# A four-layer modulated convolution: edge work of VectorE split in three, the scaled identity moved to ScalarE, the last weight set earlier

## What is computed

```python
def _layer(x, style, w, b, mw, mb, typ):
    s = style @ mw.T + mb
    weight = SCALE * w * s[:, None, :, None]
    demod = lax.rsqrt(jnp.sum(weight * weight, axis=(2, 3)) + EPS)
    weight = weight * demod[:, :, None, None]
    ...
out = x
for i, typ in enumerate(TYPES):   # ('same', 'upsample', 'same', 'downsample')
    out = _layer(out, style, weights[i], biases[i], mod_w[i], mod_b[i], typ)
x = x + out
```

## Time and profile before

| | before |
|---|---|
| median of 3 runs | 683.77 us (682.12 to 684.29) |
| the profiled execution | 683.69 us, span 681.9 us |
| TensorE matmul busy | 653.8 us (96%) |
| TensorE weight load busy | 622.7 us (91%) |
| VectorE busy | 558.8 us (82%) |
| GpSimd busy | 456.9 us (67%) |
| ScalarE busy | 354.6 us (52%) |
| chain that ended last | PE 57%, DVE 20%, issue 12%, ACT 6% |

### The profile page before, as it was taken

How to read it: one execution, slowest core, us unless ns; L and a number is a source line. 1 busy time by engine, 2 the same in 40 slices (tenths; PEclk the granted TensorE clock), 3 DMA queues, 4 the chain that set the end, 5 groups by cost and what they waited for, 6 DMA issues and landing times.

```text
span 681.9 us, 12957 instructions
## 1 busy us (share of the span) xinstructions
PE 653.8 (96%) x4771; PEld 622.7 (91%) x4771; DVE 558.8 (82%) x680; ACT 354.6 (52%) x610; POOL 456.9 (67%) x393
## 2 busy tenths in 40 slices
PE   8998999899999999998999999999989999999887
PEld 7798999899899999998989999999979899999886
DVE  6988788888898888798788888888889888888861
ACT  5354545654555655535655555566454565555441
POOL 3357677775778877657857777786577777777620
PEclk9998999999999999998999999999999999999999
DMA  7348877578778778886758888777787677988764
GB/s 251 63 102 209 209 168 198 146 196 193 173 197 193 193 192 207 197 192 171 175 165 206 213 185 201 185 187 192 175 223 172 153 196 195 216 194 205 184 170 126
DMA packets 146990, 125.63 MB, mean 184 GB/s; under 512 B 6064, under 2 KB 113648, under 8 KB 146928
## 3 DMA queue, kind: packets, MB, share of 16 engines
q1 hardware_dynamic: 146560, 124.56, 73.8%
q10 hardware_dynamic: 368, 0.25, 0.1%
HBM read 36.51 MB, written 33.75 MB: 103 GB/s over the span
## 4 chain that ended last, share of the span: by engine, by line
PE 57%; DVE 20%; issue 12%; ACT 6%; DMA 2%; SPq 1%; DVEq 0%; ACTq 0%; POOL 0%; POOLq 0%
PE po L200 9%; PE po L201 9%; PE po L202 9%; PE pg L202 4%; PE pg L200 4%; PE pg L201 4%; PE pm L200 4%; PE pm L202 4%; PE pm L201 4%; ACT xh L554 3%; DVE Wf L853 3%; DVE T L827 2%; PE pg L205 2%; PE pg L206 2%; DVE Wf L857 2%
## 5 line engine op out<-in xcount | busy, mean ns | idle before, releaser
L200 PE MATMUL po<-xh,W 128*128 128x256 f32 (+1 forms) x640 | 202.9, 317 | 7.6 <-issue 3.7
L201 PE MATMUL po<-xl,W 128*128 128x256 f32 (+1 forms) x640 | 201.7, 315 | 0.0
L202 PE MATMUL po<-xh,W 128*128 128x256 f32 (+1 forms) x640 | 200.9, 314 | 0.0
L818 DVE TENSOR_TENSOR xl<-X,xh 128x1290 fp32r<-128x1290 f32 x64 | 140.9, 2201 | 61.9 <-ACT xh L554 60.8
L200 PEld LDWEIGHTS po<-xh,W 128*128 128x128 f32 x640 | 126.9, 198 | 14.7 <-issue 9.3
L202 PEld LDWEIGHTS po<-xh,W 128*128 128x128 f32 x640 | 127.1, 199 | 6.2
L201 PEld LDWEIGHTS po<-xl,W 128*128 128x128 f32 x640 | 127.7, 200 | 5.3
L607 ACT CAST Gh<-Gf 128x512 fp32r<-128x512 f32 x64 | 39.6, 619 | 152.9 <-DVE Gf L849 152.9
L827 DVE SCALAR_TENSOR_TENSOR T<-po,DD,M 128x512 f32<-128x512 f32 x96 | 71.2, 742 | 32.2 <-ACT M L561 21.2
L750 POOL TENSOR_TENSOR Gl<-Gf,Gh 128x256 fp32r<-128x256 f32 x30 | 22.6, 754 | 103.1 <-ACT Gh L607 103.1
L554 ACT CAST xh<-X 128x1290 fp32r<-128x1290 f32 x64 | 87.8, 1372 | 7.4 <-POOL X L719 5.4
(11 more groups left out here) (175 smaller groups left out, 1786.2 us busy)
## 6 DMA issues: line engine op xcount, KB each, us to landing
X<-in_xin SPq DMA_DIRECT2D x64, 516.0 KB, 4.2
out<-T SPq DMA_DIRECT2D x64, 512.0 KB, 5.8
W<-W SPq DMA_DIRECT2D x93, 256.0 KB, 4.5
W<-W SPq DMA_DIRECT2D x31, 384.0 KB, 5.6
V<-V SPq DMA_DIRECT2D x32, 256.0 KB, 5.2
V<-W SPq DMA_DIRECT2D x32, 128.0 KB, 4.4
V<-Vx SPq DMA_DIRECT2D x32, 128.0 KB, 4.2
E<-in_ed SPq DMA_DIRECT2D x1, 768.0 KB, 7.3
```

Of the source, the lines that this page charges most:

```text
L200: eng.matmul(o, wh_, rh, start=first, stop=False)
L201: eng.matmul(o, wh_, rl, start=False, stop=False)
L202: return eng.matmul(o, wl_, rh, start=False, stop=last)
L818: tt(xl[:, n % XH, 0:w], X[:, n % XR, 0:w], r32(xh[:, n % XH, 0:w]), ALU.subtract).then_inc(s_xl, 1)
```

## The change

On VectorE, `edge` takes a third argument. Part 0 stands where all of it stood, at the end of sample 3's turn; part 1 at the end of the next group's sample 0, part 2 at the end of sample 0 another group later. On ScalarE a group's first turn begins with `x_high` of the odd tile and with the identity for the next group, then come the casts; `m_out` of sample 1 moves ahead of the cast of unit 6 (the last sum: three of W's five blocks). GpSimd loses the identity. In the table, group 29 does unit 3 of group 31 one sample earlier, and group 30 does units 4 to 6 of group 31 ahead of sample 0 instead of sample 1.

```diff
+         NGR - 3: [[(2, 0), (2, 1)], [(1, 4), (1, 5), (1, 6)], [(2, 2), (2, 3)], []],
+         NGR - 2: [[(1, 4), (1, 5), (1, 6)], [], [], []]}
...
+            def identity(g):
+                if g:
+                    act.wait_ge(s_ce, cnt(g - 1, 5))
+                for b in range(NG):
+                    m = act.activation(cols(ID[:])[:, b // 2, :, b % 2], EYE[:, 0:C], ACT.Copy,
+                                       scale=inv3[:, g * NG + b:g * NG + b + 1])
+                m.then_inc(s_id, 1)
...
             high(0, 3)
+            act.wait_ge(s_sc, SC_D)
+            identity(0)
             q3_high(1)
...
                 if i == 0:
-                    if b == 0:
-                        x_high(1)
-                    for x in units_of(b):
-                        high(*x)
-                    if b:
-                        x_high(2 * g + 1)
+                    x_high(2 * g + 1)
+                    if g + 1 < NGR:
+                        identity(g + 1)
+                    highs(b, (0, 1, 2, 3, 4, 6))
...
                     t_out(b - 1)
-                    for x in units_of(b):
-                        if x[1] != 5:
-                            high(*x)
+                    highs(b, (0, 1, 4))
                     m_out(b)
+                    highs(b, (6,))
+                    sums_behind(b)
...
-            def identity(g):
-                if g:
-                    pool.wait_ge(s_ce, cnt(g - 1, 5))
-                pool.tensor_tensor(cols(ID[:]), EYE[:, 0:C].unsqueeze(1).unsqueeze(3).to_broadcast([128, 2, C, 2]),
-                                   bc2(gs(inv3, g), 1), ALU.mult).then_inc(s_id, 1)
...
-                if divmod(b - 1, NG) in edge_at:
-                    c, k = edge_at[divmod(b - 1, NG)]
-                    edge(c, k)
-                    if k == 3 and c + 1 < len(CHUNKS):
-                        edge_in(c + 1)
+                for part, back in ((0, 1), (1, 2), (2, 6)):
+                    if divmod(b - back, NG) in edge_at:
+                        edge(*edge_at[divmod(b - back, NG)], part)
```

More of the change, by code:

```diff
@@ L41 @@
 FIRST = {0: [[(1, 2), (1, 3)], [(2, 0), (2, 1)], [(1, 4), (1, 5), (1, 6)], [(2, 2)]],
-         1: [[(1, 3), (2, 0), (2, 1)]] + SLOTS[1:]}
+         1: [[(1, 3), (2, 0), (2, 1)]] + SLOTS[1:],
+         NGR - 3: [[(2, 0), (2, 1)], [(1, 4), (1, 5), (1, 6)], [(2, 2), (2, 3)], []],
+         NGR - 2: [[(1, 4), (1, 5), (1, 6)], [], [], []]}
 def shared(b):
@@ L652, in _, with highs, sums_behind @@
             q3_high(2)
+            def highs(b, part):
+                for x in units_of(b):
+                    if x[1] in part:
+                        high(*x)
+            def sums_behind(b):
+                if weights_at(b - 1):
+                    sums_high(weights_at(b - 1))
             for b in range(B):
@@ L678, in _ @@
                 elif i == 2:
[L679 to L682, removed]
+                    highs(b, (4, 6))
                     m_out(b)
@@ L685, in _ @@
                         x_high(2)
[L686 to L690, removed]
-                else:
[L692 to L695, removed]
+                    sums_behind(b)
+                    highs(b, (2, 3))
+                else:
+                    sums_behind(b)
+                    highs(b, (2, 3))
                     m_out(b)
@@ L765, in _ @@
             pool.wait_ge(s_sc, SC_D)
-            pool.wait_ge(s_in["eye"], 16)
-            identity(0)
             q3_full(1)
@@ L778, in _ @@
                         for x in units_of(b):
-                            low(*x)
-                    if g + 1 < NGR:
-                        identity(g + 1)
+                            if x[1] < 4:
+                                low(*x)
                 elif i == 1:
@@ L897, in edge_in, with edge @@
                 tt(XS[:, 0:n], XE[:, cs, :], bc(S[:, 0, cs], 8), ALU.mult).then_inc(s_ed, 1)
-            def edge(c, k):
+            def edge(c, k, part):
                 a, n = CHUNKS[c]
@@ L903, in edge @@
                 y1, y2 = Y1[:, 0:n], Y2[:, 0:n]
[L904 to L908, removed]
-                elif k == 1:
[L910 to L914, removed]
+                if part == 0:
+                    dve.wait_ge(s_e, 4 * c + k + 1)
+                    if k == 0:
+                        v = y1[:, :, 0:6]
+                        link(tt(v, got(0, 6), bc(b0z[:, cs], 6), ALU.add))
+                        tt(ZE[:, 0:n, 1:7], v, bc(D10[:, cs], 6), ALU.mult).then_inc(s_ed, 1)
+                    elif k == 1:
+                        tt(y1[:, :, 0:11:2], got(0, 6), bc(S[:, 1, cs], 6), ALU.mult)
+                        link(tt(y1[:, :, 1:10:2], got(6, 5), bc(S[:, 1, cs], 5), ALU.mult))
+                        link(dve.tensor_scalar(Y[:, 0:n, 1:12], y1[:, :, 0:11], bias(1), None, ALU.add))
+                    elif k == 2:
+                        link(tt(y1[:, :, 0:8], got(0, 8), bc(DD[:, P2, cs], 8), ALU.mult))
+                        link(dve.tensor_scalar(HH[:, 0:n, 2:10], y1[:, :, 0:8], bias(2), None, ALU.add))
+                    else:
+                        v = y1[:, :, 0:3]
+                        link(tt(v, got(0, 3), bc(DD[:, P3, cs], 3), ALU.mult))
+                        dve.scalar_tensor_tensor(out=EP[:, cs], in0=v, scalar=bias(3), in1=XE[:, cs, 1:4],
+                                                 op0=ALU.add, op1=ALU.add).then_inc(s_ed, 1)
+                elif part == 1:
+                    if k == 1:
+                        link(tt(y1[:, :, 0:11], Y[:, 0:n, 1:12], Y[:, 0:n, 0:11], ALU.add))
+                        link(tt(y2[:, :, 0:10], y1[:, :, 1:11], y1[:, :, 0:10], ALU.add))
+                    elif k == 2:
+                        link(tt(y1[:, :, 0:9], HH[:, 0:n, 1:10], HH[:, 0:n, 0:9], ALU.add))
+                        link(tt(y2[:, :, 0:8], y1[:, :, 1:9], y1[:, :, 0:8], ALU.add))
+                    elif k == 3 and c + 1 < len(CHUNKS):
+                        edge_in(c + 1)
+                elif k == 1:
@@ L918, in edge @@
                 elif k == 2:
[L919 to L923, removed]
                     link(tt(y1[:, :, 0:7], y2[:, :, 1:8], y2[:, :, 0:7], ALU.add))
@@ L926, in edge @@
                                              op0=ALU.mult, op1=ALU.mult).then_inc(s_ed, 1)
[L927 to L931, removed]
             def final():
```

## The result

The changed kernel takes **656.56 us** (median of 4 runs, 656.35 to 656.76), the kernel before 683.42 us on the same chip. The ratio is 0.9608 with a 95% interval of 0.9592 to 0.9625. The forecast was 659.4 us and the range 654 to 671. The profiled execution took 656.46 us, 654.7 of it span.

The account below looks back on a forecast made before the run. A loop through ScalarE and VectorE, a little longer than TensorE's work, stalls TensorE. Span 681.9 less 26.3 (19.89 middle, 6.37 end) plus 2.0 staying is 657.6; 1.8 more gives 659.4 us, range 654 to 671.

Parts of the forecast that it names:

- The loop: Groups 2 to 28: M, Q2h, xh, xl and W's differences take a little longer than TensorE's work, 18.85 us.
- Its size: Groups 2 to 28: 544.48 us less 524.59 is 19.89 us of stalls; 2.0 us set against the gain.
- low end: 654 us: no residue (657.4), edge-matmul overlap (1 us) and the half-clock stretch at 59.09 gone (1.7 us).
- ScalarE's row of steps: Each group from T0 + 1.2: xh 1.39, identity 1.15, Q2h to T 3.45 us; M at T0 + 8.3.
- xl and W: VectorE in each group: xl starts at T0 + 2.9, takes 2.21 us; W's differences end at T0 + 10.1.
- Counts as nothing: GpSimd: losing 32 identity operations, median 2.02 us, gains no time, since it is on nobody's path.
- The edges: Edge groups and those behind: 4.30 us of VectorE work, split into 1.48, 1.74 and 1.08 us, fits.
- The end: After 625.31 us: stalls of 2.07, 1.76, 0.83 and 1.71 us for half clock go, 6.37 us in all.
- The loop stays, shorter: Rival, 0.13: identities cost 0.40 us each, the loop stays the bound, some 0.5 us lost a group; 671 us.
- The wait moves: Rival, 0.05: W's crossing grows by 1 us or more and the stall shows up behind it; 676 to 683 us.
- last sign of being wrong: The crossing from the end of W's differences to the next plain convolution takes 9 us.
- The slower rival: Rival, 0.04: four identities hold up ScalarE's queue; gain lost from 2.7 us for four, 697 us at 0.8 each.

Follow-up runs that it names:

- m_ahead_only: Kernel before with M ahead of the second W cast and nothing else: 683.27 us, ratio 0.9991.
- xh_behind: Changed kernel with xh again behind the casts to Q2h and the identity behind xh: 676.13 us, ratio 0.9893.
- m_behind: Changed kernel with M of the second sample again behind the cast of unit 6: 656.60 us, ratio 0.9605.
- gpsimd_identity: Changed kernel with the identity on GpSimd again: 657.32 us, ratio 0.9620.
- xh_first_only: Kernel before with ScalarE casting xh of the odd tile ahead of Q2h and the other casts, nothing else: 668.86 us, ratio 0.9787.

## Why the prediction was right, step by step

**The loop.** Right, and the main point. In the changed kernel every group from 2 to 28 takes 18.85 us plus its edge matmuls, to within 0.1 us; with xh behind Q2h, in the same kernel, 19.3 us come back in the middle (542.19 against 522.85). That the loop goes through xh, xl and W, and not through M, is shown by m_ahead_only and xh_behind together; "M" here is that of the second sample. The M of the last sample, with which the prediction's loop starts, hangs on VectorE too, through Gf and the cast to Gh; the prediction took its time as fixed.

**Its size.** The step forecast 19.89 less a residue of 2.0. Measured: 21.63. Two terms were mis-sized. The residue was 0.13 us (groups 17 and 18), as W ended earlier than I thought. And the edge matmuls cost 13.9 us (522.85 less 508.95), not 15.64: their rows sum to 15.64 us in the changed kernel too, so 1.7 us of them lie beside their neighbours. The prediction had named 1 us of this overlap for its low end. It also named one half-clock stretch among the stalls' consequences where there were two; the sum is not touched, since it took the stretch as a whole.

**ScalarE's row of steps.** Identity 1.15 forecast, 1.07 measured for four (336 to 354 ns each, overlapping). M at T0 + 8.3 forecast, 7.98 measured, and not from ScalarE's work: it waits 1.30 us for TensorE. M's term in the argument was empty, since M behind the cast costs nothing either (m_behind).

**xl and W.** W's second difference was forecast at T0 + 10.1 and ended at 9.78. Three terms were off and nearly cancel. The start was kept at T0 + 1.2, the end of the last sample's M; in group 27 that M ends at T0 + 0.27, and xl starts at T0 + 1.90 instead of 2.9. xl, kept at 2.21, takes 1.76, because it starts ahead of GpSimd's differences now, and not behind them. And the 0.6 us allowed for TensorE's sums became waits of 1.09 and 0.63 in group 27, 1.80 and 0.63 in group 26. That the end came within 0.3 us of the forecast is in part luck; what holds W at T0 + 9.78 is TensorE, which VectorE now waits for.

**GpSimd.** "Counts as nothing" was right for the changed kernel as a whole (0.8 us, gpsimd_identity) but wrong as reasoning: with xh first and the identity left on GpSimd, VectorE waits 18.4 us for it, and 10.2 us of time hang on the move. I looked at who waits for the identity in the trace of before, not at who would, once VectorE is early. The claim on the shared port held: the Trainium skill, page "SBUF — State Buffer", section "SBUF: two separate sides", has a VectorE operation with two SBUF inputs and a GpSimd operation that reads SBUF exclude each other for a whole instruction, the first to start going first. The trace agrees: the same identity instruction takes 2.02 us in the median before and 0.61 us (612 to 616 ns) in xh_first_only, where GpSimd's first difference waits instead. And xl takes 1.76 us in gpsimd_identity too, so it was not the identity that made it longer.

**The edges.** The mechanism failed. They were counted in the 19.89 us as stalls that the split removes, and alone it removes none of them on balance (685.92). xh first and the identity remove them, edges whole (658.63). The long block hurt because xh stood behind it through Q2f; once xh does not, VectorE's own wait for TensorE takes the block in. The forecast of T0 + 10.4 for W in the group after an edge was near (10.19 in group 4).

**The end.** 6.37 forecast, 4.78 measured. The stalls of 2.07 and 1.76 us and the half clock are gone, 0.83 became 0.53, but two new ones of 0.61 and 0.90 us appeared. The prediction had named up to 2 us that could return there and counted none; 1.6 us did, at the end and not in the middle, where the sum had put its residue.

**The start.** Forecast unchanged; 0.82 us shorter, and the clock behind that is no effect of the change. The stall of 2.05 us at 58.99 is still there, but the granted clock stays at 1.00 behind it, where it was 0.50 for 3.41 us before. The profiles of all 13 other kernels here have such a half-clock stretch within 1.5 us of that stall, m_behind included, whose start takes 80.37 us with it. And of the four executions of the changed kernel two have a mean clock of 1.000 (656.46 and 656.35 us) and two 0.996 (656.66 and 656.76). So the low end's term of 1.7 us for this stretch came in by the luck of the profiled execution, and the four executions differ by 0.4 us at most. A new wait for GpSimd in group 1 takes 0.54.

Together: 657.6 forecast for the span, less 3.74 in the middle, less 0.82 at the start, plus 1.59 at the end, is 654.6; measured 654.7.

**The rivals.** "The loop stays, shorter" asked for 0.40 us an identity without overlap; four take 1.07. "The wait moves" is what M ahead alone does, but not the whole change. The 9.07 us from W's end to the next plain convolution in groups 26 and 27 match the prediction's last sign of being wrong, but the sign was badly put: it measures slack. The crossing did not grow: from W's end to the landing of its last copy it takes 7.7 us in the median of the 27 groups, before and now, while DMA works 0.80 of the time instead of 0.77. The slower rival's price was wrong: it put the turning point at 2.7 us for the identity; at 2.98 us (576.31 to 579.29) the kernel still is 2.8% faster than before, since 11 groups lose 0.3 to 0.8 us each, and not 27 groups 1 us.

## What to carry to other kernels

When a loop runs through several engines, the wait that the bound engine names can be only the place where the loop closes: move the step that starts the loop (here a cast that needed nothing of what stood ahead of it), and check with one edit whether the named wait is cause or symptom. After a wait is gone, look for everything that was early only because the waiting engine was late; the next one here was an identity on an engine that nobody had waited for. Splitting a long block is no gain by itself: alone it made this kernel 0.4% slower, and after the loop was broken it was hardly needed. And a stretch that differs in clock between two profiles is to be looked up in the other executions before it is put down to the change.

## What the runs showed of the hardware

In these traces the duration that the profile gives a GpSimd or VectorE instruction with two SBUF inputs contains its wait for the other engine. xl of the same shape takes 2.21 us when it starts 0.14 us behind a GpSimd difference, and 1.76 us when it starts first; GpSimd's difference of 128x512 then takes 2.37 us (126.50, started 0.54 us behind xl) where group 26 of the changed kernel has 1.55. A busy share of GpSimd read from such rows is too high: it fell from 393.30 to 334.95 us in the middle, 58 us, though the 27 identities that left it are worth 27 x 0.61 = 16 us at their shortest.

A stall of the same length at the same place need not bring the lower clock: 2.02 us before the matmul at 59.02 is followed by 0.50 in the kernel before, and 2.05 us before the one at 58.99 by 1.00 in the changed kernel. In the other 12 profiles a stall of 2.0 to 2.4 us at this place is followed by 0.50 each time. Why is open.
